# Attention on one core: V read in place, four column groups for the sums, a ring of three score banks, transposed scores a step later

## What is computed

```
scale = 1 / sqrt(sqrt(d_head))
Q = (X @ Wq.T + bq).reshape(B, S, H, d_head) * scale      # K the same, V without scale
scores = einsum('bqhd,bkhd->bhqk', Q, K)
scores = where(causal, scores, -inf)
attn = softmax(scores, axis=-1)
out = einsum('bhqk,bkhd->bqhd', attn, V).reshape(B, S, D)
return out @ Wo.T + bo
```

## Time and profile before

| | |
|---|---|
| median of 3 runs | 2948.74 us (2948.06 to 2952.24) |
| the profiled execution | 2949.92 us, its span 2948.2 |
| TensorE | 2591.4 us busy, 88% |
| VectorE | 2095.3 us busy, 71% |
| ScalarE | 1211.8 us busy, 41% |
| GpSimd | 1139.5 us busy, 39%, nothing of it in the attention |
| mean granted clock of TensorE | 0.942 of full |

### The profile page before, as it was taken

One profiled execution on the slowest core, in us unless ns is written; L12 is line 12 of the kernel. 1 busy time (PEld: TensorE's weight loads), 2 busy tenths in 40 slices (PEclk: granted clock), 3 DMA queues, 4 the chain that ended last, 5 costly groups with the idle time before them and its releaser, 6 DMA issues. The chain is left out here.

```text
span 2948.2 us, 44171 instructions
## 1 busy us (share of the span) xinstructions
PE 2591.4 (88%) x14212; PEld 1911.2 (65%) x14212; DVE 2095.3 (71%) x3431; ACT 1211.8 (41%) x2468; POOL 1139.5 (39%) x1240
## 2 busy tenths in 40 slices
PE   4894289999999999999999943999999869999993
PEld 2783278888888888888888832888888633333322
DVE  3355678888888888888888855777777664444434
ACT  1122145555555555555555521222222234444441
POOL 0251146565665656565665521455445200000000
PEclk9997589999999999999999976999999879999996
DMA  3100200000000000000000010000000031111114
GB/s 117 42 17 31 70 2 3 28 3 28 3 3 28 3 28 3 28 3 28 3 3 3 3 58 25 18 28 26 24 24 24 25 99 36 37 37 37 37 27 96
DMA packets 82365, 83.65 MB, mean 28 GB/s; under 512 B 25120, under 2 KB 71040, under 8 KB 79904
## 3 DMA queue, kind: packets, MB, share of 16 engines
q1 hardware_dynamic: 80672, 81.48, 9.4%
q10 hardware_dynamic: 1536, 0.20, 0.0%
HBM read 62.42 MB, written 16.78 MB: 27 GB/s over the span
## 5 line engine op out<-in xcount | busy, mean ns | idle before, releaser
L734 DVE SCALAR_TENSOR_TENSOR mix_cv<-mix_pp,mix_cw,mix_cv 128x384 f32<-128x384 f32 (+4 forms) x864 | 493.0, 571 | 25.4 <-ACT mix_cv L657 4.5
L1495 DVE TENSOR_REDUCE att_tops<-att_psc 128x1 f32<-128x512 f32 (+3 forms) x384 | 202.1, 555 | 219.3 <-PE att_psc L1433 131.8
L965 POOL TENSOR_TENSOR ffn_hl<-ffn_h,ffn_hh 128x512 fp32r<-128x512 f32 x144 | 186.2, 1293 | 319.6 <-ACT ffn_hh L1023 319.6
L1470 PE MATMUL att_po<-att_pr,att_vh 128*17 128x512 f32 (+3 forms) x768 | 290.6, 489 | 0.0
L581 PEld LDWEIGHTS mix_pyd<-mix_xdt,mix_lm 128*128 128x128 f32 x2048 | 249.1, 193 | 56.7 <-issue 53.1
L1534 ACT ACTIVATE att_pr<-att_pst 128x512 f32<-128x512 f32 (+3 forms) x384 | 175.8, 489 | 250.9 <-PE att_pst L1452 247.5
L75 PE MATMUL mix_pp<-l0in_XH,mix_wx_lo 128*128 128x384 f32 (+2 forms) x576 | 238.5, 414 | 36.3 <-DVE mix_ss L723 20.2
L657 ACT ACTIVATE mix_cv<-mix_pp,mix_cb,mix_cw 128x384 f32<-128x384 f32 (+1 forms) x288 | 182.4, 633 | 210.2 <-PE mix_pp L77 210.2
L632 PE MATMUL mix_pgt<-mix_wo,mix_gt 128*128 128x256 f32 x1024 | 244.9, 382 | 2.9 <-issue 2.2
L581 PE MATMUL mix_pyd<-mix_xdt,mix_lm 128*128 128x64 f32 x2048 | 244.4, 273 | 2.5 <-DVE mix_lm L784 2.5
L520 POOL TENSOR_TENSOR mix_xdt<-mix_xtok,l_dt 128x512 f32<-128x512 f32 x128 | 133.8, 1045 | 278.8 <-ACT mix_xtok L684 278.8
(11 more groups left out here) (292 smaller groups left out, 6712.6 us busy)
## 6 DMA issues: line engine op xcount, KB each, us to landing
mix_w_raw<-in_w_in SPq DMA_DIRECT2D x8, 1280.0 KB, 5.9
ffn_raw<-in_wgu SPq DMA_DIRECT2D x56, 128.0 KB, 2.2
mix_ll<-cs SPq DMA_DIRECT2D x384, 4.0 KB
att_qs<-q SPq DMA_DIRECT2D x192, 32.0 KB
mix_wo_raw<-in_w_out SPq DMA_DIRECT2D x8, 512.0 KB, 6.7
ffn_draw<-in_wd SPq DMA_DIRECT2D x28, 128.0 KB, 2.1
q<-qkv_part SPq DMA_DIRECT2D x24, 128.0 KB, 1.9
k<-qkv_part SPq DMA_DIRECT2D x24, 128.0 KB, 1.9
```

The costliest lines, as they stand in the source:

```text
L734: last = dve.scalar_tensor_tensor(out, of, cw[:, g, ct, 3 - d:4 - d], out, ALU.mult, ALU.add)
L965: pool.tensor_tensor(hl[u % NH][:, :], h[u % 2][:, :], hh[u % NH][:, :].bitcast(F32), ALU.subtract).then_inc(lo_done, 1)
L1470: last = pe.matmul(po[half][0:DH + 1, q0 - half * 512:q1 - half * 512], vh[(a + 1) % 2][:, kt, :], pr[(a + 1) % 2][:, at:at + q1 - q0], st ...
L1495: dve.tensor_reduce(tops[o][:, col:col + 1], psc[g % 2][:, 0:end - c], AX.X, ALU.max).then_inc(mx_done, 1)
```

## The change

The attention's hardware loop is gone: 37 steps are written out, so each operand's address is a constant. With that,

- V is the stationary operand where it lies (`V[:, m, kts[r], :]`); the copies into `vh` are gone.
- The sums write one bank of 128 partitions. Its partitions 0, 32, 64 and 96 begin four groups of 17 (SHARES): the first for queries 0 to 511 (key tiles 0 to 3), the other three for queries 512 to 1023, with key tiles (0, 1), (2, 3, 7) and (4, 5, 6). They go in four rounds of up to four matmuls, one per group, at k = 2, 4 and 6 (ROUNDS; two rounds at 6). One copy of 128 x 512 replaces two of 17 x 512, and four DMAs store the groups; the three parts of the second half are added in the output stage.
- The score pieces and the turned maxima share a ring of three banks. The turning moves from k = 3 to k = 4 and lies ahead of the pieces of k = 5 in the ring.
- Transposed scores and exponentials go by key tile: 8 units of up to 1024 columns per head, in two buffers of two banks. They run three steps behind the scores instead of two, the sums four.
- Q's parts come with three DMAs instead of six, in a fifth buffer; the three rows of maxima in one, which SP issues instead of ScalarE.
- In the output stage the sums are loaded from the four groups in eight DMAs (4 MB instead of 2), VectorE adds the parts, the reciprocals are kept for channels in another order (Wo's rows are laid out to match) and spread in 16 DMAs of 64 KB instead of 128.

```diff
-    AHEAD = 4
+    NB = 5
+    STEPS = HEADS + 5
+    RING, ROWS_AT = 3, 5
+    ITEMS = []
+    for n in range(HEADS + 1):
+        ITEMS += [(n, g) for g in range(NP) if n < HEADS and PIECES[g][0] < ROWS_AT]
+        ITEMS += [(n - 1, None)] if n else []
+        ITEMS += [(n, g) for g in range(NP) if n < HEADS and PIECES[g][0] >= ROWS_AT]
+    PLACE = {item: i for i, item in enumerate(ITEMS)}
+    SHARES = ((0, (0, 1, 2, 3)), (1, (0, 1)), (1, (2, 3, 7)), (1, (4, 5, 6)))
+    ROUNDS = {2: (0,), 4: (1,), 6: (2, 3)}
...
-        psc = [s.bank(f"psc{a}") for a in range(2)]
-        pst = [s.bank(f"pst{a}") for a in range(3)]
-        po = [s.bank(f"po{half}") for half in range(2)]
-        prow = s.bank("prow", 1024, BF16)
+        psc = [s.bank(f"psc{a}") for a in range(RING)]
+        pst = [s.bank(f"pst{a}", 1024) for a in range(2)]
+        po = s.bank("po")
...
 # SP, per head
-                    for j, pq in enumerate(PART_Q):
-                        sp.dma_start(qs[a][j * DH:(j + 1) * DH, :], q3[pq, ch, tok]).then_inc(loaded[a], 16)
+                    wait(sp, st_done, QT * (m - NB + 1))
+                    for pq in range(3):
+                        rows_of = [j for j in range(len(PART_Q)) if PART_Q[j] == pq]
+                        sp.dma_start(qs[a][rows_of[0] * DH:(rows_of[-1] + 1) * DH, :],
+                                     q3[pq:pq + 1, ch, tok].to_broadcast([len(rows_of), DH, 1024])).then_inc(loaded[a], 16)
...
+                for n in range(1, STEPS):
+                    if live(n + 1):
+                        load(n + 1)
+                    if live(n - 5):
+                        m = n - 5
+                        sp.wait_ge(o_done, m + 1)
+                        for j in range(4):
+                            sp.dma_start(a_part[j, :, m % H1, m // H1, :], sums[m % 2][32 * j:32 * j + DH + 1, :]).then_inc(stored[m % 2], 16)
+                    if live(n - 1):
+                        m = n - 1
+                        sp.wait_ge(rows_kept, m + 1)
+                        sp.dma_start(qs[m % NB][KC:KC + 3, :], rows[m % 2][:, :]).then_inc(rows_in[m % NB], 16)
...
 # TensorE
+                        if live(n - 3):
+                            m, b = n - 3, (n - 3) % NB
+                            if k == 0:
+                                pe.wait_ge(rows_in[b], 16 * (m // NB + 1))
+                            wait(pe, ex_done, m * QT + k - 1)
+                            width = 1024 - k * P
+                            for c in range(0, width, 512):
+                                end = min(c + 512, width)
+                                last = pe.matmul(pst[k % 2][:, c:end], ks[b][:, k * P:(k + 1) * P],
+                                                 qs[b][:, k * P + c:k * P + end], start=True, stop=c > 0)
...
+                        for r in ROUNDS.get(k, ()) if live(n - 4) else ():
+                            m, o = n - 4, (n - 4) % 2
+                            if r == 0:
+                                pe.wait_ge(ex_done, QT * (m + 1))
+                                wait(pe, o_done, m)
+                            for j, (half, kts) in enumerate(SHARES):
+                                if r >= len(kts):
+                                    continue
+                                src, dst = cols_of(kts[r], half)
+                                last = pe.matmul(po[32 * j:32 * j + DH + 1, dst], V[:, m, kts[r], :], pr[o][:, src],
+                                                 start=r == 0, stop=r == len(kts) - 1)
...
 # ScalarE
+                            act.activation(pr[m % 2][:, AT[k]:AT[k + 1]], pst[k % 2][:, 0:1024 - k * P], ACT.Exp).then_inc(ex_done, 1)
+                        if live(n - 4) and k == 7:
...
+                            act.activation(sums[m % 2][:, :], po[:, :], ACT.Copy).then_inc(o_done, 1)
```

More of the change, by code:

```diff
@@ L1367, in attention @@
                                "st_done", "ex_done", "pv_done", "o_done"))
[L1368 to L1378, removed]
+        LOADS = 6
+        SMALL = NB + 3
         with nc.Block() as block:
@@ L1474, in step @@
                                 last.then_inc(pv_done, 1)
-                groups(pe, step)
             @block.vector
             def _(dve):
-                for a in range(AHEAD):
+                for a in range(NB):
                     dve.memset(ks[a][KC:KC + 3, :], 1.0).then_inc(small, 1)
-                dve.wait_ge(small, AHEAD)
+                dve.memset(po[:, :], 0.0).then_inc(small, 1)
                 dve.wait_ge(cin, 16)
@@ L1512, in _ @@
-                groups(dve, step)
+                half = slice(QT // 2, QT)
+                for n in range(HEADS):
+                    o = n % 2
+                    for g, (t, c, end, col) in enumerate(PIECES):
+                        dve.wait_ge(sc_done, n * NP + g + 1)
+                        dve.tensor_reduce(tops[o][:, col:col + 1], psc[PLACE[n, g] % RING][:, 0:end - c], AX.X, ALU.max).then_inc(mx_done, 1)
+                    dve.wait_ge(mx_done, (n + 1) * NP)
+                    dve.tensor_tensor(tops[o][:, half], tops[o][:, half], tops[o][:, QT:NP], ALU.max).then_inc(small, 1)
+                    dve.wait_ge(small, SMALL + 4 * n + 1)
+                    wait(dve, turned, n)
+                    dve.tensor_scalar(parts[:, 0:QT], tops[o][:, 0:QT], -1.0, None, ALU.mult).then_inc(small, 1)
+                    dve.wait_ge(small, SMALL + 4 * n + 2)
+                    dve.scalar_tensor_tensor(rest[:, :], tops[o][:, 0:QT], -1.0, parts[:, 0:QT], ALU.mult,
+                                             ALU.subtract).then_inc(small, 1)
+                    dve.wait_ge(small, SMALL + 4 * n + 3)
+                    dve.tensor_copy(parts[:, QT:2 * QT], rest[:, :]).then_inc(small, 1)
+                    dve.wait_ge(small, SMALL + 4 * n + 4)
+                    dve.tensor_tensor(parts[:, 2 * QT:], rest[:, :], parts[:, QT:2 * QT], ALU.subtract).then_inc(parts_done, 1)
@@ L1551, in _ @@
-                groups(act, step)
-def attention_out(nc, wo, bo, a_sum, a_total, r_total, X, F, out):
+                act.wait_ge(made, 1)
+                for n in range(STEPS):
+                    for k in range(QT):
+                        if live(n - 3):
+                            m = n - 3
+                            act.wait_ge(st_done, m * QT + k + 1)
+                            if k == 0:
+                                wait(act, pv_done, m - 1)
+                            act.activation(pr[m % 2][:, AT[k]:AT[k + 1]], pst[k % 2][:, 0:1024 - k * P], ACT.Exp).then_inc(ex_done, 1)
+                        if live(n - 4) and k == 7:
+                            m = n - 4
+                            act.wait_ge(pv_done, m + 1)
+                            wait(act, stored[m % 2], 64 * (m // 2))
+                            act.activation(sums[m % 2][:, :], po[:, :], ACT.Copy).then_inc(o_done, 1)
+                        if live(n - 1) and k == ROWS_AT - 1:
+                            m = n - 1
+                            wait(act, rows_in[(m - 2) % NB], 16 * ((m - 2) // NB + 1) if m >= 2 else 0)
+                            act.wait_ge(turned, m + 1)
+                            act.activation(rows[m % 2][:, :], psc[PLACE[m, None] % RING][0:3 * QT, 0:P], ACT.Copy).then_inc(rows_kept, 1)
@@ L1558, in attention_out @@
+def attention_out(nc, wo, bo, a_part, r_part, X, F, out):
     NB = T // TB
```

235 lines of the change are left out of this document (85 added, 150 removed).

## The result

The changed kernel takes 2830.56 us (median of 4 executions, 2829.76 to 2831.22), the kernel before 2949.17 (2948.06 to 2952.24): a ratio of 0.9596 [0.9579, 0.9613], 118.6 us less. The prediction said 2845 us, 103.2 less. The sign and nearly the size came out, but not by the steps foreseen: two of them were wrong, by some 70 and 60 us, in opposite directions. That the sum landed 14 us from the measurement is luck.

The account below looks back on a forecast made before the run. TensorE's stream was taken to bound the attention's full steps. Attention -100.7, start -1.0 and output stage -1.5 sum to -103.2 us from 2949.9, so 2846.7, or 2845 as median; range 2750 to 2905 us.

Parts of the forecast that it names:

- its own signs: Profile after: stint of four 512s 2.1 us, steps 11.3 us, TensorE over nine tenths busy; falls if TensorE waits for loads.
- What bounds the kernel before: Attention's full steps cost TensorE's stream; each f32 matmul is two records, four cycles per column, 7.68 us for the sums.
- The staircase: Sums over V: only one group's second record overlaps the next group's first; 5.01 us a step, 2.67 less; chance 0.56.
- Rival 1: Full overlap: all four column groups run at once, sums 2.35 us, step 8.6 us, time 2761 us; chance 0.18.
- Hidden: Attention's loads land in 7.9 us, 3.4 to spare; with stores and row transfer SP issues for 5.9 us; no cost.
- Waits (a) and (b): TensorE waits in a full step: 0.5 us for the 1024-column exponential's buffer at k = 2, 0.35 for a reduce at k = 6.
- Light steps: Three steps at the attention's start get a third bank: 7.4 us each instead of 8.7, VectorE setting the pace.
- Steps without scores: Three steps near the attention's end: 2.35 + 5.01 + 0.72 + 0.2 = 8.3 us each.
- The attention: All attention steps together: 378.3 us against 479, a gain of 100.7 us.
- Start: The start of the kernel loses three load issues: -1.0 us.
- Output stage: Loads of A +5.2 and +1.2 us, reciprocals' broadcasts -8.6, stores +0.7: sum -1.5 us, between +10 and -8.
- four last stores +0.7: Term of the output stage: the attention's four last stores add 0.7 us.

Follow-up runs that it names:

- one_store: The changed kernel with one DMA of 128 partitions storing a head's sums in place of four of 17 partitions: 2768.14 us.
- no_groups: one_store with two score banks instead of three and all sums over V on partitions 0 to 16 of two banks, without column groups: 2992.19 us.
- four_q_six: The changed kernel with Q loaded by six DMAs of 16 partitions again instead of three of 48, 32 and 16: 2777.16 us.
- early_stint: one_store with the first round of sums moved from k = 2 to k = 1: 2756.09 us.
- one_group_major: one_store with the 12 sums of a head ordered group by group in the same three stints: 2873.23 us.

## Why the prediction came out, point by point

By its own signs the forecast falls twice, though its number holds: the stint of four 512s lasts 0.99 us, not 2.1, and TensorE waits for the loads, so that it is busy 84% of a full step and not over nine tenths. The full step was forecast 2.5 us too long by the first (11.3, `one_store` has 8.78) and came out 1.89 us longer than that by the second; the errors had no reason to match.

- **What bounds the kernel before** held, and so did its price: two records per f32 matmul, four cycles a column. `no_groups` shows it: from the first narrow matmul of a stint to the next full-width one pass 3.54 and 3.10 us, and 1.41 at k = 6, 8.05 in all. The prediction's prices make it 7.68 + 3 x 0.12 = 8.04, with the change at the end of each stint; the one at its start lies ahead of the first narrow matmul.
- **The staircase failed.** "The next group's first record, which stands behind it, waits too" is not so: four records start together. Measured 2.73 us per step against 5.01 + 0.36. Rival 1's stint (0.9) and step (8.6, with `one_store` 8.78) are what the chip does. The step was argued from rows in which every matmul used the same columns. They could not tell waiting for one's turn from waiting for the array, and I took the first.
 The Trainium skill (TensorE: Matmul & The Clock Gate, Part 3) has both sentences, that distinct column groups run concurrently and that matmuls start and end in program order. The trace agrees with the first; with the second, read as one queue of records, it doesn't (0.99 us, four records from the first tenth on).
- **"Hidden" failed for loads and stores**, and nearly made up for it in the sum. Six issues, 5.9 us, 3.4 to spare: I counted SP's issues and took the landing from the trace of before. The price lay in what the DMA engines carry. At 25 GB/s the 10.67 us of a step are 267 KB; the four stores bring 136 KB to one engine. That Q's and K's loads bring it the rest, 132 KB, is worked out from theory E's assumption, which the 49 us of `four_q_six`'s full steps bear out but no row shows engine by engine. So it takes both, the stores' shape and the merged loads: spreading either gives most of the time back. The cost: 1.89 us a step, 53 us.
 The Trainium skill (DMA: Bandwidth & Descriptors, Why a DMA increments its semaphore by 16 and not by 1) states it: a transfer goes over the largest number of engines up to 16 that divides the outermost dimension of both its sides, which for 17 is 1. The trace agrees, with a share of 0.06 to 0.07 behind the last sums. I had not looked this up for the stores; the range covered for it, the reasons did not. For the stores that GpSimd issued the share was 0.31.
- **The clock** was an unforeseen part. TensorE's waits cost more than themselves: it waited 2.02 us up to 2594.34, and from 2596 to 2598 it was granted 0.50, which is 1.2 GHz. Busy time by stretch, after:
```profile
2592.00:2594.00 2.00, 0.33 (x4) 0.15 (x2) 1.86 (x6) 0.77 (x2) 0.00 (x0) 1.00 0.10 30
2594.00:2596.00 2.00, 1.66 (x9) 0.91 (x10) 0.79 (x4) 0.58 (x1) 0.00 (x0) 0.68 0.22 75
2596.00:2598.00 2.00, 2.00 (x12) 0.88 (x14) 0.72 (x2) 1.59 (x3) 0.00 (x0) 0.50 0.26 77
```
 The 32.4 us of waits in 250 are 1.38 us of a step's loss of 1.89. The other 0.5 fit the clock, by an estimate: 0.94 instead of the 1.00 of `one_store` is 0.6 us of 10.67.
- **Waits (a) and (b)** were 0.5 and 0.35 us a step; `one_store` has 7.4 / 200 x 8.78 = 0.32 for the exponential and 0.17 for the maxima. `early_stint` shows that the first was a real cost. The third bank, which the prediction left without a price in full steps, is worth 1.6 us in each.
- **Light steps** came out (7.4 said, 7.29 measured). **Steps without scores** took 6.5 us, not 8.3: ScalarE's pace, as rival 1 had it (6.4).
- **The attention** took 349.6 us (2407.1 to 2756.7), not 378.3. Without the 53 us it would have been under 300, as in rival 1 (294.3); in `one_store` it took 296.3.
- **Start:** +0.6 us instead of -1.0. The mask's load now stands behind the first head's, and VectorE waited 2.60 us for it.
- **Output stage:** "four last stores +0.7" was mis-sized: the gap grew by 8.6 us. The stage itself took 60.0 us (59.8 before), where -2.2 was expected: the store of the reciprocals stood 9.24 us behind A's 4 MB, and the broadcasts went out 0.63 us apart, not 0.46. The last broadcast came 30.0 us behind the first issue (28 said).

The sum: about -130 for the attention, +0.6 for the start, +8.6 for the gap and +0.2 for the output stage make -120, the spans' 119.8. The kernel that rival 1 describes, 2761 us, is `one_store` (2768); the change as written fell 62 us short of that by the shape of four stores, beside loads merged onto few engines.

## What to carry to other kernels

Narrow matmuls on different column groups run side by side, f32 too, and the gain is had by putting one of each group next to each other; work the stream out that way, and then look at what it uncovers. For each transfer count the engines it goes over, not only its bytes and its issue: four stores of 17 partitions cost this loop 62 us more than one of 128 with 1.9 times the bytes. And a freed bank can be worth as much as a change of the stream: 48 us here.

## What the runs showed of the hardware

- Four f32 matmuls of 128 x 17 by 512 columns, on partitions 0, 32, 64 and 96 of one bank: 0.99 us together with the change of width. On one group: 3.54 us. In two groups of 1024 columns each: 1.84 us, group behind group in the program (`one_group_major`).
- Four stores of 17 x 512 f32 (34 KB each) from SP: 25 GB/s in all and a DMA share of 0.06 to 0.07. The same from GpSimd: 70 GB/s at 0.31. One of 128 x 512: an issue of 0.42 us.
- One 17-partition store is issued in 0.22 to 2.41 us in the full steps of the changed kernel (0.85 on average), in 0.30 on average in those of `four_q_six`, and in 0.22 to 0.33 (once 0.56) in the steps without scores, where four at a time go out with pauses although the share stays at 0.07. A long issue in the queue's rows is a sign of transfers piled up behind it, not a price of the instruction. How many it takes no run here shows.
